# One SiLU tile in eight is computed with GpSimd's power instruction and VectorE's reciprocal instead of ScalarE's tanh

## The chip, the core and the metric

The kernel runs on one core of a Trainium2 chip. The metric is the device time of one execution in microseconds (us), lower is better. A core has five engines with queues of their own that run side by side and wait for each other through semaphores: TensorE (PE; PEld is its weight load), VectorE (DVE), ScalarE (ACT), GpSimd (POOL) and SyncE (SP), which here issues the DMAs.

## What is computed

The reference is one transformer layer with adaptive normalisation on x of shape (1, 4096, 256):

```
h = layernorm(x) * (1 + ca) + sa                  # ca, sa, ga, cb, sb, gb: from a small condition vector
x = x + ga * attention(h)                         # 16 heads of 16, keys = queries = values
h = layernorm(x) * (1 + cb) + sb
x = x + gb * (h + 0.5 * (silu(layernorm'(h) @ w1 + b1) @ w2 + b2))
```

Attention is the large part: 16 heads, each with 4096 x 4096 scores, all of which go through an exponential. The feed-forward part has 1024 hidden features, and each goes through silu(y) = y / (1 + exp(-y)) = 0.5 y (1 + tanh(0.5 y)). The change is about this function.

## The kernel before

**Work.** After a start stage of some 80 us the kernel walks over 8 chunks of 512 queries, and in each over 4 groups of 4 heads. One group holds 64 pairs (head, block of keys); the pairs of all groups stand in one row and are taken three at a time: such a step of three pairs is a *round*, 683 of them in all, 21 or 22 to a group.

**One round.** TensorE writes the scores of three pairs into six PSUM banks (`scores`, L835). ScalarE takes the exponential of the first two pairs straight out of PSUM (L799, 128x2048). VectorE meanwhile copies the third pair's scores into SBUF (`copy_scores`, L1020, 128x1024), and ScalarE then takes their exponential there in place (L804, 128x1024). TensorE multiplies finished probabilities with the values (`weigh`, L846). TensorE may write the next first two pairs when L799 has ended, and the next third pair when the copy has. Each engine has its instructions in the fixed order of the rounds, so what stands late in a queue delays all behind it.

**The rest of the layer rides along.** While chunk c attends, chunk c - 1 is finished: its out work for 7 chunks is cut into 40 pieces each, and a table made by `plan()` (L68 and after) puts them in rounds, mostly every other one. Pieces 0 to 7 are transposes and the projection, 8 to 23 the up products (two pieces for each of the 8 *up tiles* f of 128 hidden features by 512 tokens), 24 to 39 the down products (one piece has two of the 8 tiles f for one block t of 128 tokens). Where a round has a tanh, the plan puts an extra piece in it as long as there are pieces to place beyond the free places.

**One up tile.** TensorE's two pieces leave y in one PSUM bank. VectorE writes 0.5 (y + b) to SBUF (`take_up`, L1109, round of the second piece); ScalarE takes its tanh in the next round, between L799 and L804 (`tanh`, L793); VectorE computes (tanh + 1) * half into `hidden` in the round after (`finish_hidden`, L1113). Both sides use two buffers, f % 2. The tables TANH_IN and HIDDEN_IN hold these rounds. The eighth chunk has a tail of its own after all rounds, which uses ScalarE's Silu (L814) and isn't changed.

**Down products.** `down` (called by `out_piece`) adds up over f = 0 to 7; the first piece waits until `hidden_ready` counts the tiles that it needs.

**GpSimd** does two memsets at the start and nothing after.

Of the kernel before, what the change touches and what calls it, by code (L numbers as in the profile page):

```python
# [10 lines left out]
P = 128  # L11
BANK = 512
# [38 lines left out]
TURN_ATT, PROJECT, TURN_Z2, UP, DOWN, PIECES = 0, 2, 6, 8, 24, 40  # L51

PARTS = [(0, 2), (2, 4)]

# [19 lines left out]
def plan():  # L74
# [6 lines left out]
    for c in range(1, G):  # L81
        free = [FIRST[c * Q_GROUPS + g] + r for g in range(Q_GROUPS) for r in places(c * Q_GROUPS + g)]
        normed = FIRST[c * Q_GROUPS] + 20
        free = free[:TURN_Z2] + [at for at in free[TURN_Z2:] if at > normed]
        more, s = PIECES - len(free), 0
        for at in range(FIRST[c * Q_GROUPS], FIRST[(c + 1) * Q_GROUPS]):
            extra = at in tanhs and at not in free and more > 0
            if at in free or extra:
                pieces[at] = (c - 1, s)
                if UP <= s < DOWN and (s - UP) % DC == DC - 1:  # L90
                    tanhs[at + 1] = hiddens[at + 2] = (c - 1, (s - UP) // DC)
                s, more = s + 1, more - extra
        assert s == PIECES
# [71 lines left out]
def adaln_layer(nc, x, wq_t, wp_t, bp, gamma, beta, fc1_q, fc1_s, fc1_b, fc2_q, fc2_s, fc2_b,  # L165
# [9 lines left out]
    with ctx:  # L175
# [510 lines left out]
        def tok(name):  # L686
# [5 lines left out]
        half_in = a.take("half_in", 2 * BANK).rearrange("p (r n) -> p r n", r=2)  # L692
        half_tanh = a.take("half_tanh", 2 * BANK).rearrange("p (r n) -> p r n", r=2)
        sums_sb = a.take("sums_sb", BANK)
        inverse = a.take("inverse", GT * Q_HEADS).rearrange("p (t h) -> p t h", t=GT)
# [13 lines left out]
             "scaled", "hid_ready", "base_step", "z2_ready", "z2_turned", "fi_ready", "up_mm", "half_ready", "tanh_done",  # L709
             "hidden_ready", "down_mm", "y_ready", "y_stored", "tail_turned", "tail_in", "tail_up", "tail_hidden", "tail_down", "tail_base"))  # L710
        z2 = z1

# [25 lines left out]
        with nc.Block() as block:  # L738
# [47 lines left out]
            def _(act):  # L786
                scale = ctx.enter_context(act.register("exp_scale"))
                act.reg_load(scale, exp_scale[0:1, 0:1].bitcast(I32))

                def tanh(o, f):  # L790
                    act.wait_ge(half_ready, FT * o + f + 1)
                    wait(act, hidden_ready, FT * o + f - 1)
                    act.activation(half_tanh[:, f % 2, :], half_in[:, f % 2, :], ACT.Tanh).then_inc(tanh_done, 1)  # L793
# [12 lines left out]
                for part, (lo, hi) in enumerate(PARTS):  # L806
# [5 lines left out]
                    for f in range(FT):  # L812
                        act.wait_ge(tail_up, FT * part + f + 1)
                        act.activation(hidden[:, f, cols], ps_scores[:, f % 3, 0:width], ACT.Silu, bias=b1_col[:, f:f + 1]).then_inc(tail_hidden, 1)  # L814

            @block.tensor
            def _(pe):
# [66 lines left out]

                def down(t, f, to):
                    last = by_columns(to, hidden[:, f, t * P:(t + 1) * P], w2[:, f, :], f == 0, f == FT - 1)
                    if f == FT - 1:
                        last.then_inc(down_mm, 1)

                def out_piece(o, s):  # L890
# [29 lines left out]
                    elif DOWN <= s < DOWN + GT * FT // 2:  # L920
# [5 lines left out]
                        elif t == 2 and pair == 0:  # L926
                            pe.wait_ge(y_ready, 2 * o + 1)
                        for f in (2 * pair, 2 * pair + 1):
                            down(t, f, ps_out[:, (t % 2) * D:(t % 2 + 1) * D])

# [57 lines left out]
            def _(dve):  # L988
# [118 lines left out]
                def take_up(o, f):  # L1107
                    dve.wait_ge(up_mm, FT * o + f + 1)
                    dve.tensor_scalar(half_in[:, f % 2, :], ps_out, b1_col[:, f:f + 1], 0.5, ALU.add, ALU.mult).then_inc(half_ready, 1)  # L1109

                def finish_hidden(o, f):
                    dve.wait_ge(tanh_done, FT * o + f + 1)
                    dve.scalar_tensor_tensor(out=hidden[:, f, :], in0=half_tanh[:, f % 2, :], scalar=1.0, in1=half_in[:, f % 2, :],  # L1113
# [175 lines left out]
```

## Time and profile before

| | |
|---|---|
| Time, median of 2 runs | 2025.59 us (2025.57 to 2025.62) |
| Profiled execution: span from first to last instruction | 2023.6 us |
| ACT, PE, DVE, POOL busy | 1938.3, 1897.8, 1193.2, 1.3 us |
| Granted TensorE clock in the attention stage | full speed (1.00 of 2.4 GHz) |

The profile gives a span and no separate time for its execution; the median of the runs stands 2.0 us above that span. "Busy" counts the time in which an engine has an instruction under way; two ScalarE instructions overlap a little (the next starts 0.1 to 0.25 us before the one before it has ended in the records), so that start-to-start distances, not the durations, add up to the time. The view of instructions in order of time merges equal neighbours ("x16") and gives the duration of the merged stretch.

### The profile page before, as it was taken

To read this page: it belongs to the slowest core of one execution; us is meant where nothing else is said; L and a number is where in the kernel's file an instruction comes from. 1 tells how busy PE (TensorE), PEld (TensorE's weight loads), DVE (VectorE), ACT (ScalarE), POOL (GpSimd) and SP (SyncE) were. 2 spreads that over 40 slices of the span, in tenths; PEclk is the share of its full clock that TensorE was granted. 3 is DMA by queue.
4 is the path that set the end of the run, shared out by engine and by line. 5 is a ranking of instruction groups with operands and counts; after the bars stand their busy time and mean duration, and the time that the engine had idled before them with its cause. 6 is when DMAs were issued, how large, how long until landed. Compare 5 with 4: busy or idle time off the path is not lost.

```text
span 2023.6 us, 43276 instructions
## 1 busy us (share of the span) xinstructions
PE 1897.8 (94%) x18477; PEld 550.9 (27%) x18477; DVE 1193.2 (59%) x1632; ACT 1938.3 (96%) x1491; POOL 1.3 (0%) x6
## 2 busy tenths in 40 slices
PE   6888889999999999999999999999999999999998
PEld 5411112222222222222222222222222222222225
DVE  7446455765576555755557555765557555575545
ACT  3899999999999999999999999999999999999992
POOL 0000000000000000000000000000000000000000
PEclk9999999999999999999999999999999999999999
DMA  5541111121212212111111211111121111111100
GB/s 164 144 136 43 40 51 42 48 56 42 52 42 52 52 44 60 46 43 46 52 52 46 58 42 50 44 52 53 43 62 44 40 51 55 49 35 38 42 12 12
DMA packets 121346, 108.14 MB, mean 53 GB/s; under 512 B 21936, under 2 KB 120112, under 8 KB 120896
## 3 DMA queue, kind: packets, MB, share of 16 engines
q1 hardware_dynamic: 120400, 103.69, 19.2%
q8 instruction: 146, 2.39, 0.5%
q10 hardware_dynamic: 752, 1.67, 0.2%
q14 instruction: 48, 0.39, 0.1%
HBM read 96.49 MB, written 8.65 MB: 52 GB/s over the span
## 4 chain that ended last, share of the span: by engine, by line
ACT 78%; issue 11%; PE 6%; DVE 1%; DVEq 0%
ACT attend_probs L799 42%; ACT attend_probs L804 34%; PE attend_sums L846 2%; ACT attend_half_tanh L793 1%; PE attend_scores L835 1%; PE attend_out L854 1%; PE attend_scores L854 1%; DVE attend_probs L1020 0%; DVE attend_st L1038 0%; DVE attend_x L1014 0%; ACT attend_ffn_in L810 0%; PE attend_scores L860 0%; DVE attend_st L1219 0%; DVE z L1230 0%; DVE attend_rs L155 0%
## 5 line engine op out<-in xcount | busy, mean ns | idle before, releaser
L799 ACT ACTIVATE attend_probs<-attend_scores 128x2048 f32<-128x2048 f32 x683 | 1322.1, 1936 | 3.4 <-PE attend_scores L835 3.2
L1020 DVE COPY attend_probs<-attend_scores 128x1024 f32<-128x1024 f32 x682 | 835.1, 1225 | 701.4 <-PE attend_scores L835 692.8
L846 PE MATMUL attend_sums<-attend_probs,values 128*17 128x512 f32 x8192 | 1006.8, 597 | 0.3
L804 ACT ACTIVATE attend_probs<-attend_probs 128x1024 f32<-128x1024 f32 x682 | 762.6, 1118 | 1.2 <-DVE attend_probs L1020 1.2
L835 PE MATMUL attend_scores<-asks,keys 64*128 64x512 f16 x4096 | 562.0, 380 | 99.9 <-ACT attend_probs L799 73.6
L835 PEld LDWEIGHTS attend_scores<-asks,keys 64*128 64x128 f16 x4096 | 149.6, 94 | 711.7 <-ACT attend_probs L799 588.2
L846 PEld LDWEIGHTS attend_sums<-attend_probs,values 128*17 128x17 f32 x8192 | 174.0, 96 | 510.3 <-issue 459.1
L854 PE MATMUL attend_out<-w,hidden 128*32 128x256 f32 x1920 | 124.2, 379 | 0.0
L854 PE MATMUL attend_out<-attend_ffn_in,w 128*32 128x512 f32 x896 | 116.6, 592 | 0.0
L854 PEld LDWEIGHTS attend_out<-w,hidden 128*32 128x32 f32 x1920 | 62.0, 110 | 86.4 <-issue 64.3
L1109 DVE TENSOR_SCALAR attend_half_in<-attend_out,b_col 128x512 f32<-128x512 f32 x56 | 42.1, 751 | 16.3 <-PE attend_out L854 14.8
L854 PEld LDWEIGHTS attend_out<-attend_ffn_in,w 128*32 128x32 f32 x896 | 28.8, 110 | 64.2 <-issue 64.2
L1113 DVE SCALAR_TENSOR_TENSOR hidden<-attend_half_tanh,attend_half_in 128x512 f32<-128x512 f32 x56 | 38.2, 682 | 0.0
L793 ACT ACTIVATE attend_half_tanh<-attend_half_in 128x512 f32<-128x512 f32 x56 | 36.6, 653 | 0.0
L860 PE MATMUL attend_sums<-ident,attend_sums_sb 128*32 128x128 f32 x1024 | 34.6, 276 | 0.6
L991 DVE COPY attend_sums_sb<-attend_sums 128x512 f32<-128x512 f32 x32 | 22.1, 692 | 22.0 <-PE attend_sums L846 22.0
L403 ACT ACTIVATE start_h_feat<-start_ps,mod_col 128x512 f32<-128x512 f32 x16 | 11.5, 774 | 21.8 <-PE start_ps L451 21.8
L854 PE MATMUL attend_out<-wp,attend_att_feat 128*32 128x256 f32 x480 | 31.4, 379 | 0.0
L860 PEld LDWEIGHTS attend_sums<-ident,attend_sums_sb 128*32 128x32 f32 x1024 | 26.1, 109 | 14.9 <-DVE attend_sums_sb L991 14.8
L810 ACT ACTIVATE attend_ffn_in<-attend_scores,beta_col,gamma_col 128x256 f32<-128x256 f32 x4 | 2.0, 560 | 27.7 <-PE attend_scores L854 27.7
L854 PEld LDWEIGHTS attend_out<-wp,attend_att_feat 128*32 128x32 f32 x480 | 15.6, 110 | 22.6 <-issue 17.1
L556 DVE SCALAR_TENSOR_TENSOR start_q_parts<-start_ps,gains,start_q_parts 128x1024 f16<-128x1024 f32 x8 | 10.3, 1283 | 14.9 <-ACT start_q_parts L414 14.8
(146 smaller groups left out, 538.2 us busy)
## 6 DMA issues: line engine op xcount, KB each, us to landing
keys<-parts_dram SPq DMA_DIRECT2D x768, 64.0 KB
keys<-parts_dram SPq DMA_DIRECT2D x256, 56.0 KB
asks<-parts_dram SPq DMA_DIRECT2D x192, 64.0 KB
start_x_in<-L_attn_x SPq DMA_DIRECT2D x8, 512.0 KB, 9.6
parts_dram<-start_q_parts SPq DMA_DIRECT2D x16, 256.0 KB, 2.6
attend_x_now<-L_attn_x SPq DMA_DIRECT2D x8, 512.0 KB, 4.3
out<-base SPq DMA_DIRECT2D x16, 256.0 KB, 2.6
asks<-parts_dram SPq DMA_DIRECT2D x64, 56.0 KB
```

Source lines behind the costliest of these rows:

```text
L403: last = act.activation(h_feat[:, g % 2, k, :], ps_turn[:, k, :], ACT.Identity, bias=mod_col[:, k:k + 1], scale=mod_col[:, 2 + k:3 + k])
L793: act.activation(half_tanh[:, f % 2, :], half_in[:, f % 2, :], ACT.Tanh).then_inc(tanh_done, 1)
L799: act.activation(place(n, 2), ps_scores[:, 0:4, :], ACT.Exp, scale=scale).then_inc(exps_done, 1)
L804: act.activation(place(n + 2), place(n + 2), ACT.Exp, scale=scale).then_inc(exps_done, 1)
L835: last = pe.matmul(ps_scores[:, 2 * i + b, :], keys[rows, part % K_RING, hq, col:col + P], asks[rows, group * Q_HEADS + hq, :], start=True ...
L846: last = pe.matmul(ps_sums[32 * hq:32 * hq + E1, :], values[:, j + STEPS * b, (gg % Q_GROUPS) * Q_HEADS + hq, :], place(gg * PAIRS + Q_HEA ...
L854: last = pe.matmul(to[32 * q:32 * q + 32, :], held[:, 32 * q:32 * q + 32], moved, start=start, stop=stop)
L860: last = pe.matmul(bank[32 * q:32 * q + 32, t * P:(t + 1) * P], source(t)[:, 32 * q:32 * q + 32], ident[:, :], start=True, stop=True)
L991: dve.tensor_copy(sums_sb, ps_sums).then_inc(sums_copied, 1)
L1020: dve.tensor_copy(place(n), ps_scores[:, 4:6, :]).then_inc(copied, 1)
L1109: dve.tensor_scalar(half_in[:, f % 2, :], ps_out, b1_col[:, f:f + 1], 0.5, ALU.add, ALU.mult).then_inc(half_ready, 1)
L1113: dve.scalar_tensor_tensor(out=hidden[:, f, :], in0=half_tanh[:, f % 2, :], scalar=1.0, in1=half_in[:, f % 2, :], op0=ALU.add, op1=ALU.mul ...
```

## The change

Tile f = 0 of each of the 7 chunks (`POWER_TILE`) takes another way. VectorE writes y + b instead of half of it to a buffer of its own, GpSimd computes (1/e)^(y + b) = exp(-(y + b)) from it, and VectorE adds 1, takes the reciprocal and multiplies with y + b. ScalarE has no tanh for this tile. These last three VectorE instructions stand one round after the first down piece; the down products take the tiles in the order 1 to 7, 0 (`FINISHED`). The places of the 40 pieces are the same as before.

```
--- before.py
+++ after.py
@@ -50,6 +50,11 @@
 FIRST = [-(-gg * PAIRS // S_RING) for gg in range(GROUPS + 1)]
 TURN_ATT, PROJECT, TURN_Z2, UP, DOWN, PIECES = 0, 2, 6, 8, 24, 40
 
+
+POWER_TILE = 0
+FINISHED = [f for f in range(FT) if f != POWER_TILE] + [POWER_TILE]
+INV_E = 0.36787944117144233
+
 PARTS = [(0, 2), (2, 4)]
 
 
@@ -88,7 +93,12 @@
             if at in free or extra:
                 pieces[at] = (c - 1, s)
                 if UP <= s < DOWN and (s - UP) % DC == DC - 1:
-                    tanhs[at + 1] = hiddens[at + 2] = (c - 1, (s - UP) // DC)
+                    f = (s - UP) // DC
+                    tanhs[at + 1] = (c - 1, f)
+                    if f != POWER_TILE:
+                        hiddens[at + 2] = (c - 1, f)
+                if s == DOWN:
+                    hiddens[at + 1] = (c - 1, POWER_TILE)
                 s, more = s + 1, more - extra
         assert s == PIECES
     return pieces, tanhs, hiddens
@@ -691,6 +701,8 @@
         ffn_in = a.take("ffn_in", DC * BANK).rearrange("p (k n) -> p k n", k=DC)
         half_in = a.take("half_in", 2 * BANK).rearrange("p (r n) -> p r n", r=2)
         half_tanh = a.take("half_tanh", 2 * BANK).rearrange("p (r n) -> p r n", r=2)
+        power_in, power = a.take("power_in", BANK), a.take("power", BANK)
+        inv_e = a.take("inv_e", 1)
         sums_sb = a.take("sums_sb", BANK)
         inverse = a.take("inverse", GT * Q_HEADS).rearrange("p (t h) -> p t h", t=GT)
         st2 = a.take("st2", GT * 6).rearrange("p (t s) -> p t s", t=GT)
@@ -708,6 +720,7 @@
              "xn_in", "xb_ready", "att_turned", "af_ready", "proj_mm", "x1_ready", "n_stats", "n_mom", "n_rstd", "z1_ready",
              "scaled", "hid_ready", "base_step", "z2_ready", "z2_turned", "fi_ready", "up_mm", "half_ready", "tanh_done",
              "hidden_ready", "down_mm", "y_ready", "y_stored", "tail_turned", "tail_in", "tail_up", "tail_hidden", "tail_down", "tail_base"))
+        power_ready, power_step, inv_e_set = (sem(n) for n in ("power_ready", "power_step", "inv_e_set"))
         z2 = z1
 
         ps_scores = a.banks("scores", 2 * S_RING)
@@ -788,8 +801,10 @@
                 act.reg_load(scale, exp_scale[0:1, 0:1].bitcast(I32))
 
                 def tanh(o, f):
+                    if f == POWER_TILE:
+                        return
                     act.wait_ge(half_ready, FT * o + f + 1)
-                    wait(act, hidden_ready, FT * o + f - 1)
+                    wait(act, hidden_ready, FT * o + f - 2)
                     act.activation(half_tanh[:, f % 2, :], half_in[:, f % 2, :], ACT.Tanh).then_inc(tanh_done, 1)
 
                 for at in range(ROUNDS):
@@ -812,6 +827,14 @@
                     for f in range(FT):
                         act.wait_ge(tail_up, FT * part + f + 1)
                         act.activation(hidden[:, f, cols], ps_scores[:, f % 3, 0:width], ACT.Silu, bias=b1_col[:, f:f + 1]).then_inc(tail_hidden, 1)
+
+            @block.gpsimd
+            def _(pool):
+                pool.memset(inv_e, INV_E).then_inc(inv_e_set, 1)
+                pool.wait_ge(inv_e_set, 1)
+                for o in range(G - 1):
+                    pool.wait_ge(half_ready, FT * o + POWER_TILE + 1)
+                    pool.tensor_tensor(power, inv_e.broadcast_to([P, BANK]), power_in, ALU.pow).then_inc(power_ready, 1)
 
             @block.tensor
             def _(pe):
@@ -882,9 +905,10 @@
                     if k == DC - 1:
                         last.then_inc(up_mm, 1)
 
-                def down(t, f, to):
-                    last = by_columns(to, hidden[:, f, t * P:(t + 1) * P], w2[:, f, :], f == 0, f == FT - 1)
-                    if f == FT - 1:
+                def down(t, i, to):
+                    f = FINISHED[i]
+                    last = by_columns(to, hidden[:, f, t * P:(t + 1) * P], w2[:, f, :], i == 0, i == FT - 1)
+                    if i == FT - 1:
                         last.then_inc(down_mm, 1)
 
                 def out_piece(o, s):
@@ -925,8 +949,8 @@
                             pe.wait_ge(hidden_ready, FT * o + 2 * pair + 2)
                         elif t == 2 and pair == 0:
                             pe.wait_ge(y_ready, 2 * o + 1)
-                        for f in (2 * pair, 2 * pair + 1):
-                            down(t, f, ps_out[:, (t % 2) * D:(t % 2 + 1) * D])
+                        for i in (2 * pair, 2 * pair + 1):
+                            down(t, i, ps_out[:, (t % 2) * D:(t % 2 + 1) * D])
 
                 for gg in range(GROUPS):
                     for r, (begin, end) in enumerate(units(gg)):
@@ -1106,10 +1130,21 @@
 
                 def take_up(o, f):
                     dve.wait_ge(up_mm, FT * o + f + 1)
+                    if f == POWER_TILE:
+                        dve.tensor_scalar(power_in, ps_out, b1_col[:, f:f + 1], None, ALU.add).then_inc(half_ready, 1)
+                        return
                     dve.tensor_scalar(half_in[:, f % 2, :], ps_out, b1_col[:, f:f + 1], 0.5, ALU.add, ALU.mult).then_inc(half_ready, 1)
 
                 def finish_hidden(o, f):
-                    dve.wait_ge(tanh_done, FT * o + f + 1)
+                    if f == POWER_TILE:
+                        dve.wait_ge(power_ready, o + 1)
+                        dve.tensor_scalar(power, power, 1.0, None, ALU.add).then_inc(power_step, 1)
+                        dve.wait_ge(power_step, 2 * o + 1)
+                        dve.reciprocal(power, power).then_inc(power_step, 1)
+                        dve.wait_ge(power_step, 2 * o + 2)
+                        dve.tensor_tensor(hidden[:, f, :], power, power_in, ALU.mult).then_inc(hidden_ready, 1)
+                        return
+                    dve.wait_ge(tanh_done, (FT - 1) * o + f)
                     dve.scalar_tensor_tensor(out=hidden[:, f, :], in0=half_tanh[:, f % 2, :], scalar=1.0, in1=half_in[:, f % 2, :],
                                              op0=ALU.add, op1=ALU.mult).then_inc(hidden_ready, 1)
```

**ScalarE, around the first up tile of the first chunk.** Names: `attend_probs` the probabilities, `attend_scores` their PSUM banks, `attend_half_tanh` the tanh. Before:

```order
L804 ACTIVATE attend_probs<-attend_probs 128x1024
L799 ACTIVATE attend_probs<-attend_scores 128x2048
L793 ACTIVATE attend_half_tanh<-attend_half_in 128x512
L804 ACTIVATE attend_probs<-attend_probs 128x1024
L799 ACTIVATE attend_probs<-attend_scores 128x2048
L804 ACTIVATE attend_probs<-attend_probs 128x1024
L799 ACTIVATE attend_probs<-attend_scores 128x2048
L793 ACTIVATE attend_half_tanh<-attend_half_in 128x512
```

With the change:

```order
L819 ACTIVATE attend_probs<-attend_probs 128x1024
L814 ACTIVATE attend_probs<-attend_scores 128x2048
L819 ACTIVATE attend_probs<-attend_probs 128x1024
L814 ACTIVATE attend_probs<-attend_scores 128x2048
L819 ACTIVATE attend_probs<-attend_probs 128x1024
L814 ACTIVATE attend_probs<-attend_scores 128x2048
L808 ACTIVATE attend_half_tanh<-attend_half_in 128x512
```

The tanh of tile 0 is gone; the next one, of tile 1, stands where it stood.

**VectorE, the same place.** `attend_half_in` is the halved input of the tanh, `attend_out` the PSUM bank of the out work. Before:

```order
L1020 COPY attend_probs<-attend_scores 128x1024 x4
L1109 TENSOR_SCALAR attend_half_in<-attend_out,b_col 128x512
L1020 COPY attend_probs<-attend_scores 128x1024 x2
L1113 SCALAR_TENSOR_TENSOR hidden<-attend_half_tanh,attend_half_in 128x512
L1109 TENSOR_SCALAR attend_half_in<-attend_out,b_col 128x512
L1020 COPY attend_probs<-attend_scores 128x1024 x2
L1113 SCALAR_TENSOR_TENSOR hidden<-attend_half_tanh,attend_half_in 128x512
L1109 TENSOR_SCALAR attend_half_in<-attend_out,b_col 128x512
```

With the change:

```order
L1044 COPY attend_probs<-attend_scores 128x1024 x4
L1134 TENSOR_SCALAR attend_power_in<-attend_out,b_col 128x512
L1044 COPY attend_probs<-attend_scores 128x1024 x2
L1136 TENSOR_SCALAR attend_half_in<-attend_out,b_col 128x512
L1044 COPY attend_probs<-attend_scores 128x1024 x2
L1148 SCALAR_TENSOR_TENSOR hidden<-attend_half_tanh,attend_half_in 128x512
L1136 TENSOR_SCALAR attend_half_in<-attend_out,b_col 128x512
L1044 COPY attend_probs<-attend_scores 128x1024 x2
```

The `hidden` instruction of tile 0 is gone from here; the first that remains is that of tile 1, two rounds later.

**VectorE, from up tile 7 to the down products of the first chunk.** Before:

```order
L1109 TENSOR_SCALAR attend_half_in<-attend_out,b_col 128x512
L1020 COPY attend_probs<-attend_scores 128x1024 x2
L1113 SCALAR_TENSOR_TENSOR hidden<-attend_half_tanh,attend_half_in 128x512
L1020 COPY attend_probs<-attend_scores 128x1024 x5
L1031 TENSOR_TENSOR base<-attend_hid,mod 128x1024
L1020 COPY attend_probs<-attend_scores 128x1024 x2
```

With the change:

```order
L1136 TENSOR_SCALAR attend_half_in<-attend_out,b_col 128x512
L1044 COPY attend_probs<-attend_scores 128x1024 x2
L1148 SCALAR_TENSOR_TENSOR hidden<-attend_half_tanh,attend_half_in 128x512
L1044 COPY attend_probs<-attend_scores 128x1024
L1141 TENSOR_SCALAR attend_power<-attend_power 128x512
L1143 RECIPROCAL attend_power<-attend_power 128x512
L1145 TENSOR_TENSOR hidden<-attend_power,attend_power_in 128x512
L1044 COPY attend_probs<-attend_scores 128x1024 x4
L1055 TENSOR_TENSOR base<-attend_hid,mod 128x1024
```

Three 128x512 instructions stand now between two copies that had nothing between them. On GpSimd stand one memset of 128x1 and seven TENSOR_TENSOR 128x512, each behind a wait for `half_ready` of its chunk's tile 0.

## Rows read from the trace of the kernel before

**Rows 1.** The page: span, and busy time of each engine.

```profile
span 2023.6 us, 43276 instructions
...
PE 1897.8 (94%) x18477; PEld 550.9 (27%) x18477; DVE 1193.2 (59%) x1632; ACT 1938.3 (96%) x1491; POOL 1.3 (0%) x6
```

**Rows 2.** Waits of ACT in the attention stage (80 to 2000): us, times, longest.

```profile
ACT attend_probs L799 <- PE attend_scores L835: 3.2, 3, 1.7
...
ACT attend_probs L804 <- DVE attend_probs L1020: 1.2, 3, 0.4
```

**Rows 3.** The page's costliest groups: busy us, mean ns, idle before.

```profile
L799 ACT ACTIVATE attend_probs<-attend_scores 128x2048 f32<-128x2048 f32 x683 | 1322.1, 1936 | 3.4 <-PE attend_scores L835 3.2
...
L804 ACT ACTIVATE attend_probs<-attend_probs 128x1024 f32<-128x1024 f32 x682 | 762.6, 1118 | 1.2 <-DVE attend_probs L1020 1.2
...
L793 ACT ACTIVATE attend_half_tanh<-attend_half_in 128x512 f32<-128x512 f32 x56 | 36.6, 653 | 0.0
```

**Rows 4.** In order of time, two rounds behind the first down piece: start, us.

```profile
935.46 1.23 DVE L1020 COPY attend_probs<-attend_scores 128x1024 f32<-128x1024 f32 x1 [1.41 <-PE attend_scores L835]
...
938.17 1.23 DVE L1020 COPY attend_probs<-attend_scores 128x1024 f32<-128x1024 f32 x1 [1.49 <-PE attend_scores L835]
...
939.73 1.18 ACT L804 ACTIVATE attend_probs<-attend_probs 128x1024 f32<-128x1024 f32 x1
```

**Rows 5.** In order of time, the round with tile 0's tanh (third chunk).

```profile
864.96 0.82 PE L835 MATMUL attend_scores<-asks,keys 64*128 64x512 f16 x6
864.98 0.75 DVE L1109 TENSOR_SCALAR attend_half_in<-attend_out,b_col 128x512 f32<-128x512 f32 x1 [0.64 <-PE attend_out L854]
...
865.71 1.91 PE L846 MATMUL attend_sums<-attend_probs,values 128*17 128x512 f32 x16
...
867.38 0.75 ACT L793 ACTIVATE attend_half_tanh<-attend_half_in 128x512 f32<-128x512 f32 x1
867.43 1.04 PE L854 MATMUL attend_out<-attend_ffn_in,w 128*32 128x512 f32 x8
...
868.41 0.82 PE L835 MATMUL attend_scores<-asks,keys 64*128 64x512 f16 x6
869.05 1.88 ACT L799 ACTIVATE attend_probs<-attend_scores 128x2048 f32<-128x2048 f32 x1
```

**Rows 6.** ACT in order of time: a round without, then one with a tanh (tile 5).

```profile
898.55 1.90 ACT L799 ACTIVATE attend_probs<-attend_scores 128x2048 f32<-128x2048 f32 x1
...
901.26 1.90 ACT L799 ACTIVATE attend_probs<-attend_scores 128x2048 f32<-128x2048 f32 x1
...
904.48 1.91 ACT L799 ACTIVATE attend_probs<-attend_scores 128x2048 f32<-128x2048 f32 x1
```

**Rows 7.** DVE groups by shape: busy us, mean ns, idle before.

```profile
L1113 DVE SCALAR_TENSOR_TENSOR hidden<-attend_half_tanh,attend_half_in 128x512 f32<-128x512 f32 x56 | 38.2, 682 | 0.0
...
L997 DVE RECIPROCAL attend_inverse<-attend_sums 128x16 f32<-128x16 f32 x32 | 8.0, 251 | 1.5 <-PE attend_sums L860 1.5
...
L151 DVE TENSOR_TENSOR start_rsqrt_work<-start_rstd 128x16 f32<-128x16 f32 x3 | 0.5, 176 | 0.1
...
L1145 DVE TENSOR_SCALAR z<-mod 128x512 f32<-128x512 f32 x1 | 0.4, 420 | 0.0
...
L646 DVE TENSOR_REDUCE start_top_row<-start_ps 1x32 f32<-1x128 f32 x1 | 0.3, 278 | 0.4 <-PE start_ps L491 0.4
...
L568 DVE RECIPROCAL start_silu_c<-start_silu_c 128x2 f32<-128x2 f32 x1 | 0.2, 166 | 0.0
```

**Rows 8.** POOL groups: the largest instruction that GpSimd runs.

```profile
L388 POOL MEMSET values<- 128x512 f32 x1 | 1.0, 1001 | 0.0
```

**Rows 9.** In order of time, behind Rows 5: tile 1 is finished, tile 2 taken.

```profile
876.46 0.68 DVE L1113 SCALAR_TENSOR_TENSOR hidden<-attend_half_tanh,attend_half_in 128x512 f32<-128x512 f32 x1
...
877.91 1.23 DVE L1020 COPY attend_probs<-attend_scores 128x1024 f32<-128x1024 f32 x1
...
880.10 1.05 ACT L804 ACTIVATE attend_probs<-attend_probs 128x1024 f32<-128x1024 f32 x1
```

More of the change, by code:

```diff
@@ L51 @@
 TURN_ATT, PROJECT, TURN_Z2, UP, DOWN, PIECES = 0, 2, 6, 8, 24, 40
+POWER_TILE = 0
+FINISHED = [f for f in range(FT) if f != POWER_TILE] + [POWER_TILE]
+INV_E = 0.36787944117144233
 PARTS = [(0, 2), (2, 4)]
@@ L693, in adaln_layer @@
         half_tanh = a.take("half_tanh", 2 * BANK).rearrange("p (r n) -> p r n", r=2)
+        power_in, power = a.take("power_in", BANK), a.take("power", BANK)
+        inv_e = a.take("inv_e", 1)
         sums_sb = a.take("sums_sb", BANK)
@@ L710, in adaln_layer @@
              "hidden_ready", "down_mm", "y_ready", "y_stored", "tail_turned", "tail_in", "tail_up", "tail_hidden", "tail_down", "tail_base"))
+        power_ready, power_step, inv_e_set = (sem(n) for n in ("power_ready", "power_step", "inv_e_set"))
         z2 = z1
@@ L790, in tanh @@
                 def tanh(o, f):
+                    if f == POWER_TILE:
+                        return
                     act.wait_ge(half_ready, FT * o + f + 1)
-                    wait(act, hidden_ready, FT * o + f - 1)
+                    wait(act, hidden_ready, FT * o + f - 2)
                     act.activation(half_tanh[:, f % 2, :], half_in[:, f % 2, :], ACT.Tanh).then_inc(tanh_done, 1)
@@ L814, in _ @@
                         act.activation(hidden[:, f, cols], ps_scores[:, f % 3, 0:width], ACT.Silu, bias=b1_col[:, f:f + 1]).then_inc(tail_hidden, 1)
+            @block.gpsimd
+            def _(pool):
+                pool.memset(inv_e, INV_E).then_inc(inv_e_set, 1)
+                pool.wait_ge(inv_e_set, 1)
+                for o in range(G - 1):
+                    pool.wait_ge(half_ready, FT * o + POWER_TILE + 1)
+                    pool.tensor_tensor(power, inv_e.broadcast_to([P, BANK]), power_in, ALU.pow).then_inc(power_ready, 1)
             @block.tensor
@@ L927, in out_piece @@
                             pe.wait_ge(y_ready, 2 * o + 1)
-                        for f in (2 * pair, 2 * pair + 1):
-                            down(t, f, ps_out[:, (t % 2) * D:(t % 2 + 1) * D])
+                        for i in (2 * pair, 2 * pair + 1):
+                            down(t, i, ps_out[:, (t % 2) * D:(t % 2 + 1) * D])
                 for gg in range(GROUPS):
@@ L1108, in take_up @@
                     dve.wait_ge(up_mm, FT * o + f + 1)
+                    if f == POWER_TILE:
+                        dve.tensor_scalar(power_in, ps_out, b1_col[:, f:f + 1], None, ALU.add).then_inc(half_ready, 1)
+                        return
                     dve.tensor_scalar(half_in[:, f % 2, :], ps_out, b1_col[:, f:f + 1], 0.5, ALU.add, ALU.mult).then_inc(half_ready, 1)
                 def finish_hidden(o, f):
-                    dve.wait_ge(tanh_done, FT * o + f + 1)
+                    if f == POWER_TILE:
+                        dve.wait_ge(power_ready, o + 1)
+                        dve.tensor_scalar(power, power, 1.0, None, ALU.add).then_inc(power_step, 1)
+                        dve.wait_ge(power_step, 2 * o + 1)
+                        dve.reciprocal(power, power).then_inc(power_step, 1)
+                        dve.wait_ge(power_step, 2 * o + 2)
+                        dve.tensor_tensor(hidden[:, f, :], power, power_in, ALU.mult).then_inc(hidden_ready, 1)
+                        return
+                    dve.wait_ge(tanh_done, (FT - 1) * o + f)
                     dve.scalar_tensor_tensor(out=hidden[:, f, :], in0=half_tanh[:, f % 2, :], scalar=1.0, in1=half_in[:, f % 2, :],
```

14 lines of the change are left out of this document (10 added, 4 removed).

## The prediction

> **What bounds the kernel now.** I read the page first: ACT is busy for 1938.3 of the span's 2023.6 us, PE for 1897.8, DVE for 1193.2, POOL for 1.3 [rows 1]. Then what ACT waits for: in the whole attention stage 3.2 us for scores and 1.2 us for VectorE's copy [rows 2]. So ScalarE's stream of exponentials [rows 3] sets the time almost everywhere, and whatever makes it wait is paid in full. But PE has little less to do, and a share is an average; so I went to the instructions in order of time at the two places that the change touches. There the reader is to look for who starts late behind whom.
>
> **Removed: seven tanh.** A round without a tanh lasts 901.26 - 898.55 = 2.71 us, one with a tanh and no extra piece 904.48 - 901.26 = 3.22 us [rows 6]: a tanh costs 0.51 us of ScalarE's stream, not its 653 ns [rows 3], since instructions overlap. Seven would be 3.6 us. But tile 0's tanh stands in a round that also holds an extra up piece, and the change leaves the piece there. In that round PE runs without a gap: scores from 864.96, the weighing from 865.71, the piece from 867.43, the next scores at 868.41, which is 3.45 us; and ScalarE's next large exponential starts at 869.05, once its two pairs of scores are there [rows 5]. ScalarE with its tanh taken away would be ready about 0.7 us earlier and find no scores. The extra piece sits in tile 0's round in all seven chunks. Gain taken: 0 us; upper end 3.6 us, if PE could be earlier, which nothing in these rows allows.
>
> **Removed from VectorE: seven `hidden` instructions** of 0.68 us [rows 7] in the round after. VectorE is not what that round ends on. 0 us. That VectorE writes y + b and not its half is the same instruction with one operation less, 0.75 us as before [rows 5]: 0 us.
>
> **Added on VectorE, once a chunk: three instructions.**
> - The add of 1, SBUF to SBUF, 128x512 with a constant: 0.42 us, as the row of L1145, same shape and form [rows 7].
> - The product of two SBUF tiles: 0.68 us, as L1113 [rows 7].
> - The reciprocal of 128x512. The trace has it only small: 128x2 in 166 ns, 128x16 in 251 ns (32 of them) [rows 7]. An elementwise instruction on 128x16 takes 176 ns. The difference isn't the stride of the PSUM read: a reduction that reads 128 values at the same stride of 32 words takes 278 ns [rows 7], about 1 ns a value. So the reciprocal itself is slow per value: (251 - 166) / 14 = 6.1 ns. For 512 values that is 166 + 510 x 6.1 = 3.26 us, an estimate from these two rows. Lower end: it runs like any other 128x512, 0.68 us, if the 85 ns are a cost of PSUM and not of each value. Upper end: the 128x2 row hides part of its values in the fixed time; with a fixed time of 120 ns, 251 ns give 8.2 ns a value and 4.3 us. I take 3.26, which two rows of the very operation give.
>
> With 0.03 us for each hand-over the block is 0.45 + 3.29 + 0.71 = 4.45 us. In the third chunk it would start where the copy before it lets go, 1.14 us after the copy's start at 935.46, so at 936.60. It ends at 941.05. The next copy, which started at 938.17 and ended at 939.40, now starts at 941.05 and ends at 942.28; the small exponential behind it, which started at 939.73 [rows 4], starts at about 942.3: **2.6 us late**. ScalarE does not win it back, as it has no idle time to give. The round before has 1.4 us of idle time on VectorE, which is in this sum. No other work of VectorE stands in these two rounds in any chunk. TensorE has its next scores done earlier and only waits with ScalarE. Seven chunks: 7 x 2.6 = **18.2 us**. With the ends of the reciprocal the block costs 0.0 us (1.9 us long: copy ends 939.7, just in time) to 3.6 us, so 0 to 25 us in all.
>
> **Added on GpSimd: seven powers of 128x512.** No row shows a power, or any arithmetic on GpSimd. Lower end: its largest instruction, a memset of 512 values, 1.0 us [rows 8]. Upper end: if a power were built from elementwise passes as this kernel builds its inverse square root, 12 instructions, it would need a logarithm and an exponential, so some 24 to 48 passes of 1.0 us: 24 to 48 us. The result is needed 936.60 - 865.73 = 70.9 us later in the third chunk [rows 4, 5], and by the plan about 8 us (3 rounds) less in the tightest chunk: 63 us. So up to 63 us the power itself is hidden, and I cost it at nothing. What it runs beside is VectorE, and that is a rival.
>
> **Down products in another order:** same count, same shapes. The piece with tiles 7 and 0 comes fourth in block 0, three pieces and some 5 rounds behind the finished tile. 0 us. Setting 1/e and the first wait on GpSimd come during the first chunk: 0 us.
>
> **Sum.** 2025.6 - 0 + 18.2 = **2043.8 us** (the span would be 2041.8).
>
> **Rival 1: the power holds VectorE up.** The first VectorE instruction with two SBUF inputs behind the power's start (865.73) is `hidden` of tile 1 at 876.46, 10.7 us later. If it can't run while the power runs, VectorE stands still, and the copy of 877.91, which ended 0.96 us before ScalarE's need at 880.10 [rows 9], makes ScalarE wait. Price a chunk: T - 11.7 us, T being the power's length. At T = 24 us that is 7 x 12.3 = 86 us, with the 18 from above 2130 us; it passes 2% (40.5 us) at T = 14.9 us. In the trace of before GpSimd does nothing beside VectorE, so no row speaks for or against it. The Trainium skill does, in "SBUF — State Buffer", section "Who interferes with whom": VectorE instructions with two SBUF inputs and a GpSimd instruction that reads SBUF contend for a port pair, and whichever issues first makes the other wait for its whole length. No run here shows it yet; by that rule and T = 24 the time is the 2130 above, without it 2044. Chance 0.42, of which 0.05 has T of 12 to 15 us and stays within 2%.
>
> **Rival 2: the power is very long but holds nobody.** Then VectorE waits for it at 936.60, and the price is T - 68 us a chunk on average (63 to 71), with the copies behind it in the queue. At T = 100 us: 7 x 32 + 18 = 242 us, 2268 us. Against it: it would take four of the longest estimates above. Chance 0.05.
>
> **Rival 3, faster: the reciprocal is cheap, and ScalarE keeps the tanh's time.** The block is then 1.9 us long, the copy lands just in time, and 7 x 0.51 = 3.6 us are won: 2022 us. It decides at a block of 1.9 us, a reciprocal of 0.7 us, and needs PE to be earlier in tile 0's round. Against it stand the two reciprocal rows and the gapless 3.45 us of PE. Chance 0.06, most of it at 2022 to 2026 and so within 2%; 0.01 for more than that.
>
> **Rival 4: the change doesn't do what it says,** such as a power that finishes elsewhere on the queue. The order of instructions shows the seven powers behind one wait each; I leave it no chance of its own.
>
> **How the numbers follow.** The forecast, 2044 us, has 0.47; its own range is 2026 to 2050 by the ends of the reciprocal. Rival 1 has 0.42, spread from 2044 to well above 2200 with T. I let the range reach from 2022 (rival 3) to 2175, which is rival 1 with T = 30 us; left out are longer powers in rival 1 (about 0.15) and rival 2. Two per cent, about what a measurement of this kernel can tell from no change, is 40.5 us. Faster 0.01; within 2%: 0.47 + 0.05 + 0.05 = 0.57; slower: 0.37 + 0.05 = 0.42.
>
> **What would show it.** In the changed kernel's rows: a RECIPROCAL 128x512 of about 3.3 us; seven waits of the small exponential for VectorE's copy, about 2.6 us each, and none elsewhere; tile 0's round still about 3.4 us long with PE gapless. The power's length on POOL, and whether the first `hidden` behind its start keeps its 0.68 us and its place 10.7 us later, tell rival 1 from the forecast. A wait of VectorE for GpSimd before the add of 1 would be rival 2. The prediction is wrong in its mechanism if ScalarE waits at any other place, or if the seven rounds of tile 0 become shorter.

## The result

| | us | against before |
|---|---|---|
| before | 2025.59 (2 runs) | |
| changed kernel | 2154.12 (2153.01 to 2155.24, 2 runs) | ratio 1.0632, 95% interval 1.0601 to 1.0663 |
| forecast | 2043.8 (range 2022 to 2175) | |

The change costs 128.5 us. The measured time lies in the range, but by the mechanism to which the prediction gave 0.05 (rival 2): GpSimd's power lasts 81.9 us, longer than the 24 to 48 us that the prediction had as its upper end, and VectorE waits for it.

### The profile page after: what moved, and what is told of

Same layout as the page of the kernel before. It is cut to its first block, busy times and chain, and to the rows that moved or that the text cites. A ratio compares the mean times of both kernels' runs of the same rounds, so it can differ in the third digit from the quotient of the medians.

```text
span 2153.4 us, 43287 instructions
## 1 busy us (share of the span) xinstructions
PE 1913.1 (89%) x18477; PEld 551.4 (26%) x18477; DVE 1219.7 (57%) x1646; ACT 1936.5 (90%) x1484; POOL 574.9 (27%) x14
## 4 chain that ended last, share of the span: by engine, by line
ACT 47%; POOL 23%; issue 14%; PE 5%; POOLq 4%; DVE 2%; DVEq 0%
ACT attend_probs L814 26%; POOL attend_power L837 23%; ACT attend_probs L819 21%; POOLq L751 4%; PE attend_sums L869 2%; PE attend_scores L858 1%; PE attend_scores L877 1%; DVE attend_power L1143 1%; PE attend_out L877 1%; DVE attend_probs L1044 0%; DVE attend_power_in L1134 0%; DVE attend_power L1141 0%; ACT attend_ffn_in L825 0%; PE attend_scores L883 0%; PE attend_sums L883 0%
## 5 line engine op out<-in xcount | busy, mean ns | idle before, releaser
L869 PE MATMUL attend_sums<-attend_probs,values 128*17 128x512 f32 x8192 | 1018.4, 603 | 0.3
L837 POOL TENSOR_TENSOR attend_power<-attend_inv_e,attend_power_in 128x512 f32<-128x512 f32 x7 | 573.4, 81919 | 1353.1 <-DVE attend_power_in L1134 1353.1
L1141 DVE TENSOR_SCALAR attend_power<-attend_power 128x512 f32<-128x512 f32 x7 | 3.0, 427 | 101.3 <-POOL attend_power L837 101.3
L1136 DVE TENSOR_SCALAR attend_half_in<-attend_out,b_col 128x512 f32<-128x512 f32 x49 | 36.8, 751 | 16.0 <-PE attend_out L877 14.8
L1148 DVE SCALAR_TENSOR_TENSOR hidden<-attend_half_tanh,attend_half_in 128x512 f32<-128x512 f32 x49 | 33.4, 681 | 0.0
L808 ACT ACTIVATE attend_half_tanh<-attend_half_in 128x512 f32<-128x512 f32 x49 | 31.7, 647 | 0.0
```

Source lines behind the costliest of these rows:

```text
L837: pool.tensor_tensor(power, inv_e.broadcast_to([P, BANK]), power_in, ALU.pow).then_inc(power_ready, 1)
L869: last = pe.matmul(ps_sums[32 * hq:32 * hq + E1, :], values[:, j + STEPS * b, (gg % Q_GROUPS) * Q_HEADS + hq, :], place(gg * PAIRS + Q_HEA ...
```

## The profile after

The page of the changed kernel, beside [rows 1] and [rows 3]: the busy line, the slices of GpSimd and of the granted TensorE clock, and the chain of waits by engine.

```profile
span 2153.4 us, 43287 instructions
...
PE 1913.1 (89%) x18477; PEld 551.4 (26%) x18477; DVE 1219.7 (57%) x1646; ACT 1936.5 (90%) x1484; POOL 574.9 (27%) x14
...
POOL 0000000680009500193004900077000950029200
PEclk9999999989999799998999989998999989999899
...
ACT 47%; POOL 23%; issue 14%; PE 5%; POOLq 4%; DVE 2%; DVEq 0%
```

ScalarE is as busy as before in microseconds (1936.5 against 1938.3), but that is 90% of a longer span, and GpSimd now holds 23% of the chain. Each of its seven bursts ends where the clock line dips. The groups of the new instructions (busy us, mean ns, idle before):

```profile
L837 POOL TENSOR_TENSOR attend_power<-attend_inv_e,attend_power_in 128x512 f32<-128x512 f32 x7 | 573.4, 81919 | 1353.1 <-DVE attend_power_in L1134 1353.1
...
L1141 DVE TENSOR_SCALAR attend_power<-attend_power 128x512 f32<-128x512 f32 x7 | 3.0, 427 | 101.3 <-POOL attend_power L837 101.3
...
L1143 DVE RECIPROCAL attend_power<-attend_power 128x512 f32<-128x512 f32 x7 | 23.5, 3353 | 0.2
```

The power is 81.92 us; VectorE waits 101.3 us in all for it, just before the add of 1; the reciprocal is 3.35 us (3.26 was estimated). The waits of ScalarE in the attention stage, which answer to [rows 2]:

```profile
ACT attend_probs L819 <- DVE attend_probs L1044: 119.5, 10, 21.5
...
ACT attend_probs L814 <- PE attend_scores L858: 15.7, 18, 1.8
```

The first was 1.2 us and the second 3.2 us. Both are seen in one piece in order of time, at the place of [rows 4] in the third chunk (start, us):

```profile
906.71 81.92 POOL L837 TENSOR_TENSOR attend_power<-attend_inv_e,attend_power_in 128x512 f32<-128x512 f32 x1 [176.43 <-DVE attend_power_in L1134]
...
976.37 1.23 DVE L1044 COPY attend_probs<-attend_scores 128x1024 f32<-128x1024 f32 x1 [1.41 <-PE attend_scores L858]
...
988.66 0.43 DVE L1141 TENSOR_SCALAR attend_power<-attend_power 128x512 f32<-128x512 f32 x1 [11.07 <-POOL attend_power L837]
989.12 3.35 DVE L1143 RECIPROCAL attend_power<-attend_power 128x512 f32<-128x512 f32 x1
992.51 0.69 DVE L1145 TENSOR_TENSOR hidden<-attend_power,attend_power_in 128x512 f32<-128x512 f32 x1
993.12 1.22 DVE L1044 COPY attend_probs<-attend_scores 128x1024 f32<-128x1024 f32 x1
994.37 1.06 ACT L819 ACTIVATE attend_probs<-attend_probs 128x1024 f32<-128x1024 f32 x1 [13.50 <-DVE attend_probs L1044]
...
994.93 3.61 PE L869 MATMUL attend_sums<-attend_probs,values 128*17 128x512 f32 x16
...
999.55 1.88 ACT L814 ACTIVATE attend_probs<-attend_scores 128x2048 f32<-128x2048 f32 x1 [1.42 <-PE attend_scores L858]
```

The reader sees VectorE stand at the add behind a copy that is done, the next copy behind the whole block, and ScalarE's small exponential behind that copy, 13.5 us idle. Then comes something the prediction did not have: TensorE's 16 weighing matmuls take 3.61 us instead of the 1.91 of [rows 5], and ScalarE waits once more, 1.42 us. The stretches show why (the column behind POOL is the granted clock):

```profile
865.00:930.00 65.00, 61.53 (x586) 15.90 (x586) 44.89 (x77) 64.50 (x51) 23.29 (x1) 1.00 0.16 41
...
985.50:1002.60 17.10, 8.21 (x54) 1.73 (x54) 8.06 (x6) 6.59 (x5) 3.13 (x1) 0.56 0.00 1
```

TensorE stood idle for 12.9 us, from 981.5 to 994.4 us. The trace has the lower of its two clocks (1.2 GHz) from 983.4 to 1000.5 us, so it set in 2 us behind TensorE's last matmul and still held for 6 us of work after the stall; the second stretch shown lies mostly in this and has 0.56 on the mean. Later TensorE is back at 2.4 GHz.

**Where the 129 us are.** Round by round against before, the starts of ScalarE's large exponentials move apart by 129.1 us over the stage, all of it behind the first down piece of each chunk: 13.8 to 21.7 us in the round of the wait (119.9 us in seven chunks, which is the 101.3 us of VectorE's wait and 18.6 us for the block), and 1.2 to 1.9 us in the next round or two of each chunk, 10.7 us, where TensorE runs at the lower clock, less 1.5 us of small differences elsewhere.

## The experiments

The first three take the sum apart, the next look at the power's length and its neighbours, the last ask what a good version would be. Of each edit the lines that matter are shown; "..." stands for lines left out.

**GpSimd's power on half of the columns.** The other half of `power` is set to 1 once at the start and not renewed:

```
-  pool.tensor_tensor(power, inv_e.broadcast_to([P, BANK]), power_in, ALU.pow)
+  pool.tensor_tensor(power[:, 0:BANK // 2], inv_e.broadcast_to([P, BANK // 2]), power_in[:, 0:BANK // 2], ALU.pow)
```

> The changed kernel, but GpSimd takes the power of 256 of the 512 columns only (the other half of tile 0 is left out, its numbers are stale). Theory (the power lasts 160 ns a column whatever runs beside it, and costs nothing until VectorE needs it): the power lasts 41.0 us, ends inside the window of 63 to 71 us, VectorE doesn't wait for GpSimd, and what is left is the block of three VectorE instructions, 7 x 2.6 = 18.2 us: 2043.8 us, granted clock at full speed. Rival (GpSimd's power holds VectorE instructions with two SBUF inputs for its whole length): 7 x (41 - 11.7) = 205 us more, 2249 us. Rival (the power costs VectorE or ScalarE something by the mere running, in proportion to its length): half of the 129 us, about 2090 us.

Measured: 2043.45 us (ratio 1.0089, 1.0072 to 1.0106), 110.7 us less than the changed kernel. The group of the power, then ScalarE's wait for the copy:

```profile
L838 POOL TENSOR_TENSOR attend_power<-attend_inv_e,attend_power_in 128x256 f32<-128x256 f32 x7 | 287.8, 41118 | 1501.2 <-DVE attend_power_in L1136 1501.2
```

```profile
ACT attend_probs L819 <- DVE attend_probs L1046: 17.6, 10, 2.3
```

41.1 us is inside the window, VectorE waits for no power, and what is left is the block. A power of 41 us that held VectorE's two-input instructions up would have cost 205 us; it costs nothing that shows. Both large rivals fall. Two of the seven blocks were followed by 3.4 us at the lower TensorE clock and 0.8 us of loss each, the other five by none.

**The block alone, no power.** GpSimd's block is out, and the add reads the power's input:

```
-  dve.wait_ge(power_ready, o + 1)
-  dve.tensor_scalar(power, power, 1.0, None, ALU.add)
+  dve.tensor_scalar(power, power_in, 1.0, None, ALU.add)
```

> The changed kernel without any power: GpSimd's block is taken out, and VectorE's add, reciprocal and product read the input of the power instead (tile 0's exponential is left out). Theory: the block of 4.47 us (0.43 + 3.35 + 0.69) makes the small exponential 2.6 us late once a chunk, 2025.6 + 18.5 = 2044 us, and the same time as with half a power to 1 us. Rival (the reciprocal's time is hidden in idle time, and all of the loss comes from the wait for the power): 2025.6 us.

Measured: 2042.21 us (1.0088, 1.0071 to 1.0105). The late round is 2.54 to 2.59 us longer than before in each chunk, 17.9 us in all. With half a power the time is 1.2 us more; the two stretches of lower clock would make 1.5 us of it, but the runs of either kernel scatter by 2 us and more, so this difference is not shown. The block's 18 us are real, and a power that ends in time costs nothing that the runs can tell.

**The tanh gone, nothing in its place.** As the block alone, but with one product instead of the three instructions:

```
-  dve.tensor_scalar(power, power, 1.0, None, ALU.add).then_inc(power_step, 1)
...
-  dve.reciprocal(power, power).then_inc(power_step, 1)
...
-  dve.tensor_tensor(hidden[:, f, :], power, power_in, ALU.mult).then_inc(hidden_ready, 1)
+  dve.tensor_tensor(hidden[:, f, :], power_in, power_in, ALU.mult).then_inc(hidden_ready, 1)
```

> The changed kernel with no power and no block: tile 0 has no tanh on ScalarE, no GpSimd, and VectorE does one 128x512 product in place of the three instructions (tile 0's silu is left out). It gives what the removal of seven tanh is worth by itself. Theory (TensorE sets the length of tile 0's round): 0 us, 2025.6 us, tile 0's rounds still 3.35 to 3.45 us long. Rival (ScalarE sets it): 7 x 0.51 = 3.6 us less, 2022.0 us.

Measured: 2025.08 us against 2025.31 (0.9999, 0.9989 to 1.0008). Tile 0's rounds are 3.35 to 3.45 us long, as before. The same place as [rows 5], ScalarE and TensorE in order of time:

```profile
865.61 2.00 ACT L814 ACTIVATE attend_probs<-attend_scores 128x2048 f32<-128x2048 f32 x1
...
867.37 1.18 ACT L819 ACTIVATE attend_probs<-attend_probs 128x1024 f32<-128x1024 f32 x1
867.43 1.04 PE L869 MATMUL attend_out<-attend_ffn_in,w 128*32 128x512 f32 x8
868.41 0.82 PE L850 MATMUL attend_scores<-asks,keys 64*128 64x512 f16 x6
869.05 1.88 ACT L814 ACTIVATE attend_probs<-attend_scores 128x2048 f32<-128x2048 f32 x1 [0.50 <-PE attend_scores L850]
```

The small exponential follows at once, and ScalarE is then idle for 0.50 us until the scores are there: 869.05, the same start as with the tanh. The saved time has turned into a wait for TensorE.

**The piece moved out of tile 0's round,** on top of the kernel with the tanh gone:

```
-  extra = at in tanhs and at not in free and more > 0
+  extra = at in tanhs and tanhs[at][1] != POWER_TILE and at not in free and more > 0
```

> As the kernel with the tanh gone alone, and the plan puts no extra piece into tile 0's round: it goes to a later tanh round instead. Theory (TensorE's piece was what kept tile 0's round long): tile 0's rounds fall from 3.35 to 3.45 us to 2.71 us, seven other rounds grow from 3.22 to 3.33 us: 7 x (0.68 - 0.11) = 4.0 us less, 2021.6 us. Rival (the round was long for another reason): no change against the kernel with the tanh gone alone.

Measured: 2021.59 us (0.9983, 0.9974 to 0.9993), 3.5 us less than with the tanh gone alone. ScalarE's rounds at the place of [rows 5]:

```profile
863.79 2.00 ACT L814 ACTIVATE attend_probs<-attend_scores 128x2048 f32<-128x2048 f32 x1
...
865.56 1.18 ACT L819 ACTIVATE attend_probs<-attend_probs 128x1024 f32<-128x1024 f32 x1
...
866.51 2.00 ACT L814 ACTIVATE attend_probs<-attend_scores 128x2048 f32<-128x2048 f32 x1
```

Tile 0's rounds are 2.70 to 2.71 us now, and the stage is 3.85 us shorter than before. With the run above it shows that the piece was what kept the round long. The 3.85 us are the gain of the lost tanh and of the new plan together; the run of the plan alone, below, takes them apart.

**A multiplication instead of the power.**

```
-  pool.tensor_tensor(power, inv_e.broadcast_to([P, BANK]), power_in, ALU.pow)
+  pool.tensor_tensor(power, inv_e.broadcast_to([P, BANK]), power_in, ALU.mult)
```

> The changed kernel with one word changed: GpSimd multiplies instead of taking the power (tile 0's exponential is replaced by a product), so only the length of its instruction differs. Theory (all of the loss beyond the block is the power's length): GpSimd's instruction lasts 1 to 3 us, no wait for it, 2043 us as with the block alone, clock at full speed but for single short stretches. Rival (a wait of VectorE on GpSimd costs by itself, whatever its length): above 2050 us.

Measured: 2044.39 us (1.0094, 1.0078 to 1.0109). The group on GpSimd:

```profile
L837 POOL TENSOR_TENSOR attend_power<-attend_inv_e,attend_power_in 128x512 f32<-128x512 f32 x7 | 7.3, 1040 | 1741.8 <-DVE attend_power_in L1134 1741.8
```

1.04 us with the same operands and the same wait: the power itself is 79 times as long, and nothing about using GpSimd costs time here. As with half a power, two short stretches of lower clock stand behind the blocks of the fourth and the seventh chunk.

**Another base,** 1 instead of 1/e:

```
-INV_E = 0.36787944117144233
+INV_E = 1.0
```

> The changed kernel with base 1 instead of 1/e (every power is 1, so tile 0's silu is halved): one look at whether the length hangs on the values. Theory (it doesn't, since seven powers of different data lasted 81.917 to 81.927 us): 81.9 us, about 2153 us. Rival (work per value hangs on the base or the exponent): clearly shorter, and the time falls by 7 us for each us.

Measured, one run: 2153.95 us, each power 81.916 to 81.922 us. The length doesn't hang on the base, nor on the data of the seven chunks.

**The wait without the block.**

```
   dve.wait_ge(power_ready, o + 1)
-  dve.tensor_scalar(power, power, 1.0, None, ALU.add).then_inc(power_step, 1)
...
-  dve.reciprocal(power, power).then_inc(power_step, 1)
...
   dve.tensor_tensor(hidden[:, f, :], power, power_in, ALU.mult).then_inc(hidden_ready, 1)
```

> The changed kernel with the full power and its wait, but without the add and the reciprocal (the silu of tile 0 is only exp(-y) times y): one 128x512 product behind the wait. Theory (block and wait add up on VectorE's queue): each chunk's stall is 3.8 us shorter than in the changed kernel, 7 x 3.8 = 26.5 us less: 2127.5 us, with waits of 10 to 18 us a chunk and the TensorE clock still lowered behind them. Rival (the block ran in the shadow of something else, and only the wait counts): 2154 us.

Measured: 2126.3 us (1.0498, 1.0480 to 1.0516), 27.8 us less than the changed kernel. Wait and block add up: the stall of the third chunk falls from 13.75 to 9.90 us, the others likewise by 3.8 to 3.9.

**VectorE beside the power.** For tiles 5, 6 and 7 one instruction more, while the power is under way:

```
+  if f > 4:
+      dve.tensor_scalar(spare, half_in[:, f % 2, :], 1.0, None, ALU.add)
```

> The changed kernel with one more VectorE instruction for each of tiles 5, 6 and 7, while GpSimd's power runs: a 128x512 add of a constant from SBUF to SBUF, which took 0.42 us where GpSimd stood still. Theory (a power under way holds nobody up): 0.42 us each, the power still 81.9 us, the time within 3 us of 2154. Rival (this form of VectorE instruction shares a port with GpSimd, as two-input ones seemingly do not): the first of them stands still until the power ends, some 50 us a chunk, 2154 + 7 x 38 = 2420 us or so; or, if it breaks into the power, the power grows.

Measured, one run: 2152.39 us. The groups of the power and of the added instruction:

```profile
L838 POOL TENSOR_TENSOR attend_power<-attend_inv_e,attend_power_in 128x512 f32<-128x512 f32 x7 | 573.4, 81918 | 1351.1 <-DVE attend_power_in L1135 1351.1
...
L1150 DVE TENSOR_SCALAR attend_spare<-attend_half_in 128x512 f32<-128x512 f32 x21 | 8.8, 417 | 0.0
```

417 ns beside a power, 420 ns where GpSimd stood still [rows 7], and the power has its old length. Neither waits for the other.

**The last steps in four quarters,** one a round behind the first down piece, and the power in four instructions of 128 columns:

```
+  for q in range(POWER_PARTS):
+      lasts[at + 1 + q] = (c - 1, q)
...
+  for q in range(POWER_PARTS):
+      part = slice(q * PART, (q + 1) * PART)
+      pool.tensor_tensor(power[:, part], inv_e.broadcast_to([P, PART]), power_in[:, part], ALU.pow)
```

> The whole power and the whole silu of tile 0, but in four quarters of 128 columns: four power instructions, and VectorE does one quarter's add, reciprocal and product in each of the four rounds behind the first down piece. Theory (power 160 ns a column; a quarter's steps are 0.2 + 0.95 + 0.28 us and fit into VectorE's idle 1.5 us of a round): the block costs 0. The last quarter is wanted 3 rounds (8.1 us) later than the whole was, so VectorE waits 82 - 71 = 11 us in two chunks, 5.5 in three, 2.9 in two, each less 0.4 of slack: 41 us, and some us of lowered TensorE clock behind the longer waits: about 2071 us. Rival (the wait is not a matter of the date at which the result is wanted): about 2154 - 18 = 2136 us.

Measured: 2080.4 us (1.0270, 1.0253 to 1.0287), 9 us above the expectation. The groups of a quarter, and VectorE's waits for GpSimd:

```profile
L841 POOL TENSOR_TENSOR attend_power<-attend_inv_e,attend_power_in 128x128 f32<-128x128 f32 x28 | 579.4, 20716 | 1283.5 <-DVE attend_power_in L1138 1283.5
...
L1152 DVE RECIPROCAL attend_power<-attend_power 128x128 f32<-128x128 f32 x28 | 26.7, 953 | 1.0
...
DVE attend_power L1150 <- POOL attend_power L841: 50.0, 7, 11.7
```

The block costs nothing now: the rounds of the first three quarters are as long as before, and only the round of the last one stalls, by 3.5, 6.1 or 11.3 us, 47.8 us in all. Expected were 41: four quarters last 82.9 us and not 81.9, since each has its own fixed time. The rest is lower TensorE clock, 7 us where the expectation had 4. The date at which the result is wanted is thus what counts: asked for 8 us later in each chunk, the power is waited for 50.0 us instead of 101.3.

**A version meant to beat both.** 384 columns by power, the other 128 by tanh, a third of the power's columns finished in each of three rounds, and the piece moved. All of tile 0 now comes halved to SBUF, and GpSimd's base is exp(-2) in place of 1/e:

```
+  act.activation(half_tanh[:, 0, REST], power_in[:, REST], ACT.Tanh).then_inc(tanh_done, 1)     # REST = slice(384, 512)
```

> A version meant to beat both: GpSimd takes the power of 384 of tile 0's 512 columns in three instructions (61.5 us, inside the 63 us window), ScalarE takes the tanh of the other 128, VectorE finishes one part a round, and the plan puts the extra piece of tile 0's round into a later tanh round. The output is the reference's. Theory: as the kernel with tanh gone and piece moved (2021.6 us), plus 7 tanh of 128 columns at 0.2 us: 2023.0 us. Rival (parts of 1.5 us on VectorE don't fit and make the copy late by 0.1 us or more each): 21 parts x 0.1 to 0.5 us more, 2025 to 2033 us.

Measured: 2024.06 us against 2025.93 (0.999, 0.998 to 0.9999), span 2021.4 against 2023.6. No wait of VectorE for GpSimd, no late copy. In order of time on VectorE, the first part in the first chunk, the copy behind it and the start of the second part:

```profile
463.51 0.22 DVE L1158 TENSOR_SCALAR attend_power<-attend_power 128x128 f32<-128x128 f32 x1
463.76 0.95 DVE L1160 RECIPROCAL attend_power<-attend_power 128x128 f32<-128x128 f32 x1
464.75 0.29 DVE L1162 SCALAR_TENSOR_TENSOR hidden<-attend_power,attend_power_in 128x128 f32<-128x128 f32 x1
465.08 1.23 DVE L1052 COPY attend_probs<-attend_scores 128x1024 f32<-128x1024 f32 x1
466.22 0.22 DVE L1158 TENSOR_SCALAR attend_power<-attend_power 128x128 f32<-128x128 f32 x1
```

A part of 1.5 us fills the gap between two copies to the last: the copies keep their 2.71 us.

**The plan alone,** the kernel before with the same line of the plan changed and all eight tanh on ScalarE:

```
-  extra = at in tanhs and at not in free and more > 0
+  extra = at in tanhs and tanhs[at][1] != 0 and at not in free and more > 0
```

> The kernel before, with all eight tanh on ScalarE and no power; only the plan is changed: no extra piece in tile 0's round, it goes to a later tanh round. It says how much of the best try's gain belongs to the plan. Theory (a round with tanh and without piece is 3.22 us by ScalarE, with piece 3.33 to 3.45 by TensorE): tile 0's rounds 3.35 to 3.45 -> 3.22, seven others 3.22 -> 3.33: 7 x (0.17 - 0.11) = 0.4 us less, 2025.2 us; the other 2 us of the best try are the tanh work that GpSimd took. Rival (the plan is the whole gain): 2023.0 us.

Measured: 2025.06 us against 2025.15 (1.0000, 0.9991 to 1.0009); its stage is 1.0 us shorter in the trace, the best try's 2.6 us, and that of the kernel with tanh gone and piece moved 3.85 us. Tile 0's rounds are 3.22 us with the plan alone, 2.90 us in the best try. So by the traces some 1 us of the best try's gain is the plan's and some 1.6 us GpSimd's; by the medians it is 0.1 and 1.8 us. Taken off the gain with tanh gone and piece moved, the plan's share leaves 2.9 us by the traces and 3.6 us by the medians for the seven tanh, once the piece has moved. All of these are at the edge of what the runs can tell, and the best try is about 0.1% faster than before, with an interval that ends just below 1.

## Why the prediction was wrong

**The step that failed** is the one on GpSimd's powers: "Upper end: ... 24 to 48 passes of 1.0 us: 24 to 48 us. ... So up to 63 us the power itself is hidden, and I cost it at nothing." The window was right: 63 to 71 us were read, and the waits of 11.1 to 19.0 us fit 81.9 us against it. The length was not. I had no row of any arithmetic on GpSimd and built an upper end out of an analogy (passes like those of VectorE's inverse square root), at the speed of a memset. Measured are 20.7, 41.1 and 81.9 us for 128, 256 and 512 columns, 159 ns a column and 0.3 us fixed, where a multiplication takes 1.0 us for 512. The true power costs 79 such passes. So a term that was put at nothing is worth 101.3 us of waits and some 11 us of lower TensorE clock behind them. An end that rests on an analogy is no end; the design itself had one sharp edge, 63 us, and the chance of lying beyond it should have been far more than 0.05. The prediction held this chance small because T = 100 us "would take four of the longest estimates above", which is a slip: it is two of the longest, 48 us, and four of the shortest, and to pass the edge of 63 us it takes only 1.3 of the longest.

**That the time lies in the range is luck.** The range was drawn up to 2175 us for rival 1 with T = 30 us; the forecast's own mechanism had 2026 to 2050 us, and rival 2 was left out of it.

**Rival 2's price** was nearly right: (T - 68) x 7 + 18 with T = 81.9 gives 115 us, so 2141. The remaining 13 us are the lower TensorE clock behind each stall (11 us), for which the prediction had no term, and a mean window of 67.4 us rather than 68 (4 us), as the 101.3 us of waits say: (7 x 81.9 - 101.3) / 7; small differences elsewhere take off 1.5 us.

**Rival 1 was wrong.** In 81.9 us a power runs beside seven `hidden` instructions with two SBUF inputs, 49 in all. They last 680 to 684 ns, and the first of them starts 10.6 to 10.7 us behind the power's start, as it would have without one. The Trainium skill, "SBUF — State Buffer", section "Who interferes with whom", says that such an instruction and a GpSimd instruction that reads SBUF contend for a shared port pair, which the one that issues first holds for its whole length. With this power, which reads and writes SBUF, the traces here don't agree. The measurement decides: no holding up, for two-input instructions or for the one-input form of the experiment. Why the rule didn't bite here is open. The prediction gave this rival 0.42, and that weight was missing at rival 2.

**The block's price was right.** 18.2 us were forecast; the block alone measures 17.9 us in the rounds and 16.9 us in the time, the reciprocal 3.35 us against 3.26. Reading the cost per value from two small instances of the same operation worked, and so did the count of what stands behind the block on VectorE's queue.

**The tanh's worth was right.** 0 us, against the 3.6 us that seven tanh take in ScalarE's stream. The run with the tanh alone gone shows the wait of 0.5 us that took its place (the prediction had said about 0.7 us), and the run with the piece moved shows what it would take to win the time. Rival 3 fell on both of its conditions.

**Down products in another order** cost nothing that shows: the run with the tanh gone alone has the new order and the old time.

## What to carry to other kernels

Before work moves to an idle engine, measure one instruction of it there: the whole verdict on this change hung on a length of which no row spoke, and the distance to the first reader, 63 us, was the number to compare it with. An asynchronous result should be waited for late and in small parts, because a wait in an engine's fixed queue also holds what does not need the result; here VectorE's copies, and through them ScalarE. And what an instruction is worth is read in its own round: seven tanh of 0.5 us were worth nothing while TensorE's piece stood in the same round.

## What the hardware showed unexpectedly

- GpSimd's power: 159 ns a column of 128 partitions, whatever the base or the data; 81.916 to 81.927 us for 128x512 in 28 instances of four kernels. A multiplication of the same shape: 1.04 us.
- VectorE's reciprocal: 953 ns for 128 and 3353 ns for 512 columns, so 6.25 ns a column; for 512 columns that is nearly eight times the add of 1, which took 427 ns.
- Behind 34 of the 35 stalls of 3.5 to 22 us in five kernels with a whole power, in which TensorE was idle for 2.7 to 20.8 us, there is a stretch of 3.4 to 24 us with the lower level of 1.2 GHz, and it cost 0.5 to 1.9 us a time. The one without it is the sixth chunk of the kernel in quarters (stall 3.5 us); its third chunk has the same stall and was followed by one. Behind the shorter stalls of the block, in which TensorE was idle for 1.7 us, it happened in some chunks only: in two of seven with half a power and with the multiplication, in none with the block alone, although the stalls were the same 2.6 us. Why there and not in the others is open; no run here was made to settle it.
- A power under way and VectorE's instructions did not disturb each other in any trace. Whether other GpSimd instructions do was not tried.
